# A two-layer graph network on one core: a larger scratch memory for GpSimd's transfers, and a set-up buffer laid over loop operands

## The reference

```python
def layer0(node_attr, edge_index, edge_sh, edge_feat, ...):
    h = relu(edge_feat @ W1 + b1)
    w_000, w_011, w_101, w_110 = (h @ W2 + b2).reshape(e, 4, 8, 8)   # by path
    s_e, v_e = s[src], v[src]
    m0 = ALPHA * (einsum('ei,eio->eo', s_e * sh0, w_000) + C110 * einsum('eim,em,eio->eo', v_e, sh1, w_110))
    m1 = ALPHA * (einsum('ei,em,eio->eom', s_e, sh1, w_011) + einsum('eim,eio->eom', v_e * sh0, w_101))
    return segment_sum([m0, m1], dst) + SI_SCALE * (node_attr @ si)
def layer1(features, abs_distances, rel_vec, edge_index, ...):
    R = relu(abs_distances[:, None] @ w1 + b1) @ w2 + b2             # weights of 7 paths, 8 x 8
    Y = spherical_harmonics(rel_vec); Fj = features[src]
    msg = sum over paths of norm * einsum('euv,ef,evi,ofi->euo', R, Y, Fj, C)
    return zeros.at[dst].add(msg)
x = layernorm(x + layer0(x, ...))
x = layernorm(x + layer1(x, ...))
```

## Time and profile before

| | us |
|---|---|
| median of 3 runs | 4162.87 |
| lowest and highest | 4162.75, 4166.69 |
| the profiled execution | 4169.84 |
| its span, first to last instruction | 4168.0 |

### The profile page before, as it was taken

The page is one execution under the profiler, slowest core; times in us unless marked ns, Lnnn a source line. Parts: engine busy times, 40 slices in busy tenths (PEclk is TensorE's granted clock), DMA queues, the critical chain, the costliest instruction groups (busy, mean ns, idle before and its releaser), DMA issues.

```text
span 4168.0 us, 76267 instructions
## 1 busy us (share of the span) xinstructions
PE 3391.4 (81%) x23178; PEld 1952.9 (47%) x23178; DVE 3469.6 (83%) x5246; ACT 2181.1 (52%) x6573; POOL 3004.4 (72%) x3143
## 2 busy tenths in 40 slices
PE   5777777777777777777459999999999999999995
PEld 3444444444444444444235555555555555555553
DVE  8888788888878888887759988888888888888887
ACT  3555555555555555555336655555555555555553
POOL 5777777777777777777277777777777777777772
PEclk7888888888888888888779999999999999999998
DMA  3111111111111111111212212122121212121212
GB/s 104 33 30 33 29 35 33 29 33 29 33 29 35 33 29 33 29 33 29 34 35 44 47 37 47 37 47 46 38 48 37 47 37 47 37 47 37 47 37 31
DMA packets 220966, 159.83 MB, mean 38 GB/s; under 512 B 125489, under 2 KB 194994, under 8 KB 220466
## 3 DMA queue, kind: packets, MB, share of 16 engines
q0 software_dynamic: 100352, 51.58, 8.6%
q1 hardware_dynamic: 84946, 90.16, 8.4%
q10 hardware_dynamic: 35650, 17.88, 1.6%
HBM read 148.94 MB, written 10.43 MB: 38 GB/s over the span
## 4 chain that ended last, share of the span: by engine, by line
POOL 42%; issue 25%; DVE 15%; PE 7%; DMA 7%; DVEq 2%; POOLq 0%; SPq 0%; ACT 0%; ACTq 0%
POOL rows L364 42%; PE red L687 4%; DVE prod L977 3%; DMA src<-in_src 3%; PE wps L674 2%; DMA rows<-in_x,src 2%; DMA rows<-x_rows,src 2%; DVE prod L983 1%; DVE q L1032 1%; DVEq L1060 1%; DVE q L1042 1%; DVE prod L970 1%; PE wps L667 1%; DVE table L1056 1%; DVE rest L998 0%
## 5 line engine op out<-in xcount | busy, mean ns | idle before, releaser
L364 POOL DMA_INDIRECT rows<-x_rows,src x1568 | 1509.8, 963 | 569.4 <-issue 564.9
L364 POOL DMA_INDIRECT rows<-in_x,src x1568 | 1493.8, 953 | 508.5 <-issue 494.6
L687 PE MATMUL red<-prod,ident 128*128 128x336 f32 (+1 forms) x4704 | 1492.2, 471 | 0.0
L687 PEld LDWEIGHTS red<-prod,ident 128*128 128x128 f32 x4704 | 883.0, 193 | 626.5 <-issue 180.9
L667 PE MATMUL wps<-bias_parts,ones 64*128 64x448 bf16 (+1 forms) x2352 | 479.8, 405 | 694.3 <-DVE prod L977 490.8
L983 DVE TENSOR_TENSOR prod<-wps,q 128x896 f32<-128x896 f32 x784 | 835.1, 1082 | 185.3 <-PE wps L674 168.2
L493 ACT ACTIVATE gap<-iota,slot_plan 128x128 bf16<-128x128 f32 x3136 | 935.6, 386 | 7.0
L674 PE MATMUL wps<-w_sb,hidden 64*128 64x448 f32 (+1 forms) x3920 | 753.6, 480 | 0.0
L511 ACT ACTIVATE sums<-red 128x336 f32<-128x336 f32 (+1 forms) x294 | 136.3, 464 | 1082.3 <-PE red L687 1081.7
L667 PEld LDWEIGHTS wps<-bias_parts,ones 64*128 64x128 bf16 x2352 | 115.3, 95 | 1230.7 <-DVE prod L977 607.2
L674 PE MATMUL wps<-w_oi,hidden 64*128 64x256 f32 (+1 forms) x2352 | 533.5, 579 | 0.0
(11 more groups left out here) (126 smaller groups left out, 3205.6 us busy)
## 6 DMA issues: line engine op xcount, KB each, us to landing
mlp<-in_dist SPq DMA_DIRECT2D x196, 256.0 KB
mlp<-in_feat SPq DMA_DIRECT2D x98, 256.0 KB
rows<-in_x,src POOLq DMA_INDIRECT x1568
rows<-x_rows,src POOLq DMA_INDIRECT x1568
frames<-frame ACTq DMA_DIRECT2D x49, 144.0 KB, 1.8
geo<-frames ACTq DMA_DIRECT2D x98, 72.0 KB
src<-in_src SPq DMA_DIRECT2D x196, 8.0 KB
geo<-in_sh ACTq DMA_DIRECT2D x98, 32.0 KB, 1.7
```

Source lines behind the costliest of these rows:

```text
L364: nc.gpsimd.indirect_dma_start(out=rows[z][:, t, :], out_offset=None, in_=table_rows, in_offset=bass.IndirectOffsetOnAxis(ap=src_sb[z][:, ...
L687: ins = nc.tensor.matmul(red[:, bank * 512:bank * 512 + cols], ident[:], pr[:, i, :, a:b, :], start=(i == 0), stop=(i == MUL - 1))
```

## The change

```diff
-        work = sb("work", [P, 8 * GROUP])
+        arena = sb("arena", [P, 2 * TILES * 9 * MUL + 2 * RING * TILES * PATHS[1] * MUL])
+        work = arena[:, 0:8 * GROUP]
...
-        q_sb = slots(lambda z: sb(f"q{z}", [P, TILES * PATHS[1] * MUL]))
+        turned_end, paths_end = TILES * 9 * MUL, TILES * PATHS[1] * MUL
+        t_a, t_b = (arena[:, a * turned_end:(a + 1) * turned_end] for a in range(2))
+        q_sb, sums = ([arena[:, 2 * turned_end + (a * RING + z) * paths_end:2 * turned_end + (a * RING + z + 1) * paths_end]
+                       for z in range(RING)] for a in range(2))
...
-        sums = slots(lambda z: sb(f"sums{z}", [P, TILES * PATHS[1] * MUL]))
-        t_a = sb("t_a", [P, TILES * 9 * MUL])
-        t_b = sb("t_b", [P, TILES * 9 * MUL])
...
-    nc = bacc.Bacc("TRN2", target_bir_lowering=False, num_devices=1)
+    nc = bacc.Bacc("TRN2", target_bir_lowering=False, num_devices=1, dynamic_dma_scratch_size=32768)
```

## The result

The changed kernel takes **4115.1 us** (median of 4 runs, 4114.2 to 4118.6) against 4164.4 us for the kernel before beside it: a ratio of 0.9882 with an interval of 0.9867 to 0.9897, or 49 us. I had forecast 4156.1 us, in a range of 4148 to 4168. The profiled execution spans 4113.7 us against 4168.0.

The account below looks back on a forecast made before the run. GpSimd's stream of gathers was taken to set the end in both layers. Of 45.5 us in 26 long gaps, 6.8 us of waiting would go and 38.7 us of work stay: 4162.87 - 6.8 = 4156.1 us, range 4148 to 4168.

Parts of the forecast that it names:

- What bounds the kernel, and where the idle time sits: GpSimd's gathers set the end in both layers; 45.5 us over the normal gap sit in 26 long gaps.
- Part 1, the wait part: In the 26 gaps, the wait for a chunk's last landing goes, covered by one further gather: 6.8 us less.
- Part 2, the work part: In the 26 gaps, giving back places costs 13.3 ns a gather, however often GpSimd stops: 38.7 us remain.
- the sum's own bounds: Landing waits stay, 4163; or work is cheaper, beginning under the previous gather, and fewer gathers are returned, 4152.
- B: Rival: half as many returns by GpSimd, price per gather; 35.8 us remain, 9.7 us less, 4153.2; chance 0.13.
- C: Rival: half as many returns by GpSimd, price per return; 17.9 us remain, 27.6 us go, 4135.3; chance 0.13.
- The assumed second limit: A count of outstanding transfers between 113 and 227 keeps GpSimd's returns about as frequent; the sum moves by 2.9 us.
- Part 3, what is late next: DVE and PE of layer 1 have over 36 us of room, so the end gains GpSimd's gain in full.
- Part 4, the work buffer: The buffer over t_a, t_b and q, written in set-up and normalize, costs nothing, hidden by DVE's own order.
- D: Rival: the scratch setting doesn't reach the chip; gaps stay after 113 and 112 gathers, 4162.9; chance 0.06.
- E: Rival: layer 0's gathers lengthen by meetings with DVE, 21.6 us, less 6.8: 4177.7; chance 0.10.

Follow-up runs that it names:

- the arena alone: The change without its last line, so scratch memory at its default, against the kernel before: 6889.5 us against 6890.9, ratio 1.0004.
- the stripped kernel: The kernel before cut to one layer's gathers, an ACT copy and a DVE reduction, without messages, scatters and normalizations; default scratch: span 2195.0 us.
- The experiment with 114 places: The gathers-only kernel with 16512 bytes of scratch memory instead of the default: span 2194.7 us against 2195.0.
- the 127-gather run: The gathers-only kernel with 32768 bytes of scratch and 127 gathers a chunk in 12 chunks, 1524 gathers: span 2134.1 us.

## Why the prediction was wrong

- **What bounds the kernel, and where the idle time sits.** Right. The 45.5 us in 26 gaps, the count of 113 and 112, the wait for the landing of the last gather but one, and the fixed time up to the next gather hold. The 26 gaps were back with the arena alone, and the 13 of one layer in the stripped kernel, 1.775 us from landing to next gather at each.
- **Part 1, the wait part** (6.8 us go). The rule was right in kind: each further gather behind the awaited one takes 1.25 us off. But it is the whole gap from which it takes, not the wait alone.
- **Part 2, the work part** (38.7 us stay). This is the step that failed. Its price per gather was well chosen: 13.3 ns predicted, 11.7 ns and 0.47 us a return measured. What was wrong is the place I gave it. I let the 1.49 us stand in GpSimd's stream whatever was queued, because in the trace of before nothing is made meanwhile. Nothing is made because only one gather is left behind the awaited landing, and it is finished before the landing comes. The experiment with 114 places shows the other case: a gather is made while the places are given back. Part 1 said that one more gather covers the wait; by the sum above, three behind the landing cover wait and work. The term was 38.7 us, and all that is left of the 45.5 is 0.2 + 0.2. I had not carried the cover over from part 1 to part 2, but for half a sentence among the sum's own bounds, and no rival of mine did: B and C halve the number of returns and leave 35.8 and 17.9 us of their price in the stream.
- **The assumed second limit.** Borne out, 128 as far as the 127-gather run tells, and on that reading it decides which remainder counts: 128 = 8 x 16, the awaited landing is that of gather 112, and 16 gathers stand behind it. But it doesn't bear out what I drew from it, that returns as often as now leave the price where it is. No run shows the prediction's 227 gathers for twice the room; the room measured makes it 226 to 228, and the one count at 32768 bytes that the runs show is the 128 of the 127-gather kernel. Had memory been the only limit, and 227 = 14 x 16 + 3 its places, the estimate by the rule above is 1.4 + 0.47 + 224 x 0.0117 - 3 x 1.25 = 0.74 us a gap, 0.44 over a normal one, and 12 of them 5 us. A single gap of 0.39 us where 0.30 is normal, after the 128th gather of the changed kernel's layer 1, fits the limit: the semaphore records have the sequencer only 2 gathers ahead there, so that little covered a return, and 11 ahead at the 128th of layer 0, where there is no gap. I haven't tested it.
- **Part 3, what is late next.** Right: the gathers' 53 us reached the end in full, since DVE still waited for rows in 66 of 92 chunks of layer 1.
- **Part 4, the work buffer.** Nothing speaks against "nothing": the arena alone gave 1.0004, though not at GpSimd's pace, and 17408 bytes without the arena give 0.9889 (0.9873 to 0.9906) where the whole change gives 0.9882 (0.9867 to 0.9897), which can't be told apart.
- **Rivals.** B and C are out, since nothing is left of the price. D is out (the gaps went with the setting, and not with the arena). E is out: gathers of layer 0 average 945 ns after, 949 before. Gathers over 945 ns lost 8 us of that excess, a part of the gain with which I had not reckoned; that these were meetings with DVE, made fewer because the gaps no longer shift the phase of the gathers against it, is my reading, not shown.
- **Range.** 4148 to 4168 left out C at 4135 and had nothing below it. A bound "the work costs nothing at all" would have been 4162.87 - 45.5 = 4117.4, within 2.3 us of what came. Whether the work is hidden was the one unknown that no row settled. I bounded the number of returns, and let the hiding take off a few us at most (4152).

## What to carry to other kernels

When GpSimd issues many indirect DMAs, look for gaps at a fixed count of them. How much room there is matters less than how many gathers stand behind the landing that is awaited when it runs out: keep that at three or more (by the sum above; 2 left 0.69 us, and with 8 or 17 there was no gap) by the size of the scratch memory (a little more, or even less, so that it isn't one above whole chunks) or by spreading a chunk over more semaphores, which costs no memory. This pays where GpSimd sets the pace: where it didn't, the kernels without gaps were 1.7 to 2.7% slower. And if a price is seen only where an engine has nothing else queued, ask whether it would show at all with work queued; take "fully hidden" as one end of its range.

## What the runs showed of the hardware that was not expected

- The places are given back while later gathers are made: gather 114 runs from 150.00 to 150.94 us inside a return that lasts from 149.85 to 151.63. The trace's semaphore records show the lead: in the steady stretches of the kernels before and after, GpSimd's sequencer passes a chunk's waits mostly 11 gathers (9 to 12) before the chunk's first gather is made, and in layer 1 of the arena run, where GpSimd is kept waiting, none before it.
- A return costs 0.47 us and 11.7 ns a gather behind the awaited landing, but 23.3 to 23.6 ns a gather where all landings are long past and nothing is queued. That one pass over the gathers goes ahead of the landing and one behind it would give the factor of two; I haven't tested it.
- The landing that is awaited goes by the semaphores, as the counts of 112 and 96 returned gathers say. With two of 16 gathers it is the last gather of the chunk before, with four of 8 it is 17 gathers back.
- In the 127-gather kernel at most 128 gathers were outstanding, by the places of its 11 stops, with memory for 226 to 228 by the room measured.
- The stripped kernels change their pace. The expectation had been 1.25 us throughout. For the first 195 gathers or so a gather starts every 1.25 us, then the mean becomes 1.400 us: 32 gathers take 44.80 us in round after round, whatever their gaps, and in the 127-gather kernel on average. GpSimd's line in two windows of 140 us of the stripped kernel with the default size, 60 to 200 and 1060 to 1200 us:

```profile
L73 POOL DMA_INDIRECT rows<-in_x,src x111 | 104.7, 943 | 35.4 <-issue 35.4
...
L73 POOL DMA_INDIRECT rows<-in_x,src x100 | 104.6, 1046 | 36.9 <-issue 36.9
```

  111 gathers become 100. The full kernel keeps 1.25 us in both windows (112 and 113 gathers with four semaphores). What sets the 1.4 us I don't know; it hides the gaps in these spans, which is why the default size and 16512 bytes end within 0.3 us of each other there, and it leaves the single gaps as the evidence.
